# First attention of a two-layer model: VectorE multiplies the keys by their cosine straight from the PSUM banks, and the pooled keys are transposed and copied later

## The reference, cut to what matters

```
kv = x @ w_kv                                  # 256 x 1024 for each sequence
kv = kv * cos + rotate_half(kv) * sin          # rotary positions, on keys and values alike
local keys = values = layernorm(kv over a head's 64) * lng + lnb
p = softmax(kv @ w_proj over 16 tokens)        # pooling inside 16 segments of 16 tokens
pooled = layernorm(sum(p * kv over a segment)) # 16 pooled keys/values per head
out = softmax(q @ [pooled, local].T, masked) @ [pooled, local]
```

## Time and profile before

| what | value |
|---|---|
| median of 3 runs | 1521.95 us (1512.76 to 1534.51) |
| the profiled execution | 1513.62 us, span 1511.8 us |
| PE busy | 1200.5 us (79%) |
| DVE busy | 931.4 us (62%) |
| ACT busy | 822.3 us (54%) |
| POOL busy | 725.5 us (48%) |

### The profile page before, as it was taken

How to read it: one execution, slowest core, us unless ns; L and a number is a source line. 1 busy time by engine, 2 the same in 40 slices (tenths; PEclk the granted TensorE clock), 3 DMA queues, 4 the chain that set the end, 5 groups by cost and what they waited for, 6 DMA issues and landing times. The chain is left out here.

```text
span 1511.8 us, 30131 instructions
## 1 busy us (share of the span) xinstructions
PE 1200.5 (79%) x9299; PEld 928.5 (61%) x9299; DVE 931.4 (62%) x2122; ACT 822.3 (54%) x2181; POOL 725.5 (48%) x750
## 2 busy tenths in 40 slices
PE   3368988989889993898899899889937887888436
PEld 1245665656656662898899889889913444444336
DVE  4687787787876533744744664764434677776633
ACT  1256777767677771676676666666612443344101
POOL 2646748567485312565566556556653323211223
PEclk8589999989998995999999999999966999899558
DMA  7500000000000003303003000000063445331145
GB/s 221 174 2 3 1 10 3 8 10 0 9 2 8 10 8 127 124 11 125 8 11 120 16 9 10 12 12 7 10 174 81 84 87 104 58 48 21 23 121 152
DMA packets 152775, 76.43 MB, mean 51 GB/s; under 512 B 99992, under 2 KB 143384, under 8 KB 152408
## 3 DMA queue, kind: packets, MB, share of 16 engines
q1 hardware_dynamic: 144696, 66.42, 16.8%
q0 software_dynamic: 3072, 6.31, 1.3%
q10 hardware_dynamic: 4896, 2.36, 0.5%
HBM read 54.77 MB, written 19.76 MB: 49 GB/s over the span
## 5 line engine op out<-in xcount | busy, mean ns | idle before, releaser
L1477 POOL TENSOR_TENSOR hl<-hid,hh 128x256 fp32r<-128x256 f32 x396 | 294.0, 744 | 218.8 <-ACT hh L1454 215.1
L1520 DVE SCALAR_TENSOR_TENSOR hid<-GU,gub,sg 128x256 f32<-128x256 f32 x396 | 190.5, 482 | 194.7 <-ACT sg L1448 123.5
L1348 PE MATMUL GU<-xh,wh 128*128 128x256 f32 x792 | 233.3, 295 | 39.4 <-DVE wl L1496 30.3
L1448 ACT ACTIVATE sg<-GU,gub 128x256 f32<-128x256 f32 x396 | 188.1, 475 | 123.6 <-PE GU L1350 121.7
L1349 PE MATMUL GU<-xl,wh 128*128 128x256 f32 x792 | 225.3, 284 | 0.0
L1350 PE MATMUL GU<-xh,wl 128*128 128x256 f32 x792 | 225.1, 284 | 0.0
L1348 PEld LDWEIGHTS GU<-xh,wh 128*128 128x128 f32 x792 | 152.1, 192 | 49.0 <-issue 27.3
L1454 ACT CAST hh<-hid 128x256 fp32r<-128x256 f32 x396 | 158.2, 399 | 25.8 <-DVE hid L1520 25.3
L1349 PEld LDWEIGHTS GU<-xl,wh 128*128 128x128 f32 x792 | 152.5, 193 | 0.0
L1350 PEld LDWEIGHTS GU<-xh,wl 128*128 128x128 f32 x792 | 152.2, 192 | 0.0
L648 ACT ACTIVATE prob<-prob,rZ 128x272 f32<-128x272 f32 (+1 forms) x256 | 98.9, 462 | 60.6 <-DVE rZ L1021 55.2
(11 more groups left out here) (312 smaller groups left out, 2842.6 us busy)
## 6 DMA issues: line engine op xcount, KB each, us to landing
raw<-in_expert_w SPq DMA_DIRECT2D x4, 2688.0 KB, 12.0
late<-in_w SPq DMA_DIRECT2D x20, 256.0 KB, 6.1
raw<-in_expert_w SPq DMA_DIRECT2D x4, 1152.0 KB, 6.1
list<-zero SPq DMA_DIRECT2D x4, 1024.0 KB, 8.6
modb<-mod_d SPq DMA_DIRECT2D x9, 384.0 KB, 4.3
early<-rel_d SPq DMA_DIRECT2D x1, 3072.0 KB, 13.1
qkv_d<-qkv SPq DMA_DIRECT2D x48, 64.0 KB
early<-in_w SPq DMA_DIRECT2D x12, 256.0 KB, 4.2
```

The source lines that it names most:

```text
L1348: pe.matmul(out, lhs[0], rhs[0], start=start, stop=False, skip_group_check=True)
L1448: act.activation(sg[:, c % BUFS], GU[c % BUFS][:, 0:TT], ACT.Silu, bias=gub[:, GATE, e * CH0 + c:e * CH0 + c + 1]).then_inc(silu, 1)
L1477: pool.tensor_tensor(hl[:, b], hid[:, b], hh[:, b].bitcast(F32), ALU.subtract).then_inc(hid_lo, 1)
L1520: dve.scalar_tensor_tensor(out=hid[:, c % BUFS], in0=GU[c % BUFS][:, TT:2 * TT], scalar=gub[:, UP, e * CH0 + c:e * CH0 + c + 1], in1=sg[:, ...
```

## The change

Bank by bank, DVE now makes the cosine product from PSUM, after ACT has copied the bank, and it is this product that drains the bank. ACT's copy signals a new semaphore `kv_out`, for which DVE and POOL wait. `kvraw` stays as the source of POOL's sine product. The instruction of 1024 columns becomes two of 512. In `hp` 6, DVE does `kv_cosine` of the second tokens first, then `kv_rotate` of the first, then `pooled_keys` (before: pooled keys, rotate, cosine). PE's transpose of the pooled keys moves from ahead of the value products to directly ahead of `kT0, kT1`. The wait of `kv_rotate` for `kv_a` is replaced by one for the drained banks.

```diff
                             if k == 0 and not known_zero(r):
                                 act.wait_ge(kv_r, 2 * r + t - 1)
-                            act.copy(kvraw[:, t, k * 512:(k + 1) * 512], a[:]).then_inc(bank.drained, 1)
+                            act.copy(kvraw[:, t, k * 512:(k + 1) * 512], a[:]).then_inc(kv_out, 1)
...
             def kv_cosine(slot, b, t):
 
+                if not known_zero(b):
+                    dve.wait_ge(wk_done, 2 * b)
+                for k, (bank, a) in enumerate(((bank0, A0), (bank1, A1))):
+                    dve.wait_ge(kv_out, 4 * b + 2 * t + k + 1)
+                    bank.wait_full(dve, f"kv{t}{k}", slot)
+                    dve.tensor_tensor(heads_of(kvr[:, t, k * 512:(k + 1) * 512]), heads_of(a[:]),
+                                      cst("cosk")[:, None, t * DH0:(t + 1) * DH0].broadcast_to([P, H0 // 2, DH0]),
+                                      ALU.mult).then_inc(bank.drained, 1)
+
+            def kv_rotate(slot, b, t):
                 bank0.wait_emptied(dve, f"kv{t}0", slot)
                 bank1.wait_emptied(dve, f"kv{t}1", slot)
-                if not known_zero(b):
-                    dve.wait_ge(wk_done, 2 * b)
-                dve.tensor_tensor(heads_of(kvr[:, t, :]), heads_of(kvraw[:, t, :]),
-                                  cst("cosk")[:, None, t * DH0:(t + 1) * DH0].broadcast_to([P, H0, DH0]),
-                                  ALU.mult).then_inc(kv_a, 1)
-
-            def kv_rotate(b, t):
-                dve.wait_ge(kv_a, 2 * b + t + 1)
                 dve.wait_ge(kv_rot, 4 * b + 2 * t + 2)
...
PE's order:
-                    if early and hp == 6:
-                        gkT_mm(slot, slot + 1)
                     if early and hp == 7:
                         for c in (2, 3):
                             kT_mm(slot, slot + 1, np_, c)
...
                     if early and hp == 6:
+                        gkT_mm(slot, slot + 1)
                         for c in (0, 1):
                             kT_mm(slot, slot + 1, np_, c)
...
DVE's order:
+                    if norm and hp == 6:
+                        kv_cosine(slot, r, 1)
+                        kv_rotate(slot, r, 0)
                     if early and hp == 6:
                         pooled_keys(slot, b, np_)
-                    if norm and hp == 6:
-                        kv_rotate(r, 0)
-                        kv_cosine(slot, r, 1)
...
             def swap_rotate(slot, b, t):
-                bank0.wait_emptied(pool, f"kv{t}0", slot)
-                bank1.wait_emptied(pool, f"kv{t}1", slot)
+                pool.wait_ge(kv_out, 4 * b + 2 * t + 2)
```

More of the change, by code:

```diff
@@ L300, in layer0_attention @@
         ln_rstd = sem("ln_rstd")
-        kv_rot = sem("kv_rot")
-        kv_a = sem("kv_a"); kv_r = sem("kv_r"); kv_mean = sem("kv_mean"); kv_c = sem("kv_c")
+        kv_rot = sem("kv_rot"); kv_out = sem("kv_out")
+        kv_r = sem("kv_r"); kv_mean = sem("kv_mean"); kv_c = sem("kv_c")
         kv_sq = sem("kv_sq"); kv_ss = sem("kv_ss"); kv_norm = sem("kv_norm")
@@ L1064, in slot_program @@
                         choose(slot, l)
+                    if norm and hp == 6:
+                        kv_cosine(slot, r, 1)
+                        kv_rotate(slot, r, 0)
                     if early and hp == 6:
                         pooled_keys(slot, b, np_)
-                    if norm and hp == 6:
-                        kv_rotate(r, 0)
-                        kv_cosine(slot, r, 1)
                     if norm and hp == 7:
-                        kv_rotate(r, 1)
+                        kv_rotate(slot, r, 1)
                         kv_center(r, 0)
```

## The result

| | before | after |
|---|---|---|
| median of the runs, us | 1524.68 (1512.76 to 1534.51, 4 runs) | 1559.87 (1552.09 to 1561.7, 4 runs) |
| profiled execution, us | 1513.6 | 1561.7 |
| span, us | 1511.8 | 1559.9 |
| mean granted clock of PE | 0.896 | 0.876 |

After over before is 1.0234, with a 95% interval of 1.0187 to 1.0281: slower by 2.3%, 35.2 us by the medians. The forecast was +23.3 us. The sign and the mechanism came out as predicted, 1559.87 lies in the range, and the size is 12 us short.

The account below looks back on a forecast made before the run. No engine is full; a ring of short steps bounds the first attention, DVE late in steps 6 and 7. Terms 12.5 + 0.9 + 0.9 + 0.5 + 8.5 = 23.3 us gave 1545.3 us, range 1526 to 1567.

Parts of the forecast that it names:

- The cosine product: DVE, steps 5 and 6: pair from PSUM never stretched, 1.29 us; 0.1 us more in step 5, 2.1 us less in step 6.
- The bank held longer: PE at the router, slots 1 to 5: waits 4.4 us for DVE to drain bank1; step 6 begins 2.6 us late.
- Step 7: PE's second wait, at kT0 for the pooled-key copy, uses up DVE's 2.1 us relief; 2.4 us of lateness remain.
- (c): Rival: clock falls for the whole chain after the router and again after PE's second wait; +45, 1567 us; chance 0.27.
- slot 0: No router; kv10 and kv11 wait for the cosine pair, costing step 6 about 0.5 us; 0.9 us in all.
- slots 1 to 5: Loop slots: 2.5 us of waits each, 12.5 us, plus 1.7 us of low clock each behind the router, 8.5 us.
- Start-up: Before the loop: pooled-key copy 5.9 us later, against gains of 2.1, 1.0 and 2.3; 0.5 us, between -2 and +3.
- slot 6: No cosine; pooled keys' transpose and copy stand between the transposes of the probabilities and kT0: 0.9 us.
- (a): The forecast itself, waits plus low clock in the first attention: +18 to +30 us; chance 0.45.
- (b): Rival: waits as forecast, but PE's clock stays up or falls where PE has slack; +15, 1537 us; chance 0.20.
- (d): Rival: late router covered by DVE's choose, so DVE's relief stands alone; -16 us, 1506 us; chance 0.05.
- (e): Rival: product waits in DVE's queue where nothing gets ready earlier, PE had other slack; about 0, 1522 us; chance 0.03.

Follow-up runs that it names:

- filler: Changed kernel plus 32 PE transposes of a constant into a free bank ahead of the router, slots 1 to 5; 1.0134 to the kernel before, 1539.1 us.
- first_only: Kernel before with only the first tokens' cosine product (step 5) taken from PSUM and draining its banks, old orders; 1.0124, 1538.4 us.
- early_mid: Changed kernel, first rotation behind pooled keys, step 5 product ahead of maxima, step 6 product between maxima and rotated queries; 0.9839 to the kernel before, 1495.2 us.
- order_only: Kernel before with only the change's new order of step 6, products still from ACT's copy in SBUF; 1.0209, 1552.7 us.
- early_sooner: Changed kernel, first rotation behind pooled keys, step 5 product ahead of the maxima, step 6 product left in place; 0.9878 to the kernel before, 1500.7 us.
- keys_sooner: Changed kernel with the first rotation moved behind the pooled keys in step 6; 1.0082 to the kernel before, 1530.0 us.
- second_only: Kernel before with only the second tokens' cosine product (step 6) from PSUM, and the change's order of step 6; 1.0227, 1552.0 us.

## Why the prediction was right in sign and short in size

**The cosine product: right.** All 32 instructions of the changed line, and the add of the rotation, in the changed kernel:

```profile
L818 DVE TENSOR_TENSOR kvr<-A,const x32: 673/680/692, 25.5 to 478.4; 128x512 f32<-128x512 f32 x32
L826 DVE TENSOR_TENSOR kvr<-kvr,kvs x16: 1208/1216/3246, 30.6 to 488.2; 128x1024 f32<-128x1024 f32 x16
```

692 ns at most against 3358 ns before. The Trainium skill's rule (SBUF — State Buffer, Who interferes with whom) that an operation of VectorE with at most one SBUF input is not shut out by GpSimd is borne out by the first row; the add, with two, still goes up to 3246. Three of the 32 start at 59.76, 61.40 and 63.28 us, inside a product of POOL on `V` (L1153, 59.48 to 64.15 us), and take 0.69 us each.

**The bank held longer: right.** Forecast 4.4 us of wait at the router, measured 4.23. The step from the router to the scores of step 6 was 6.2 us by the forecast and is 8.34 (334.58 + 1.07 - 327.31): the difference, 2.1 us, is the low clock. `filler` shows the two parts apart: 2.4 us for the wait, where I had 2.6, and 2.2 for the clock, where I had 1.7. `first_only` has the held bank alone and loses 1.2%, and `early_mid` drains from DVE as well, but promptly, and gains. "Evacuate promptly" is the advice of the Trainium skill (PSUM — Partial Sum Buffer, Summary: rules for kernel authors), with the small size of PSUM as its reason. These runs agree with the advice, but for another reason: the next writer of the bank had the path behind it.

**Step 7, the mis-sized term.** The forecast had the second wait at about 2.6 us, measured 2.47, and it had the copy of the pooled keys 6.5 us after the maxima of step 6 done, measured 6.3. What failed is the next sentence: "`kT0` and `kT1` ... 0.93, scores 1.46", 2.4 us, and with it the sentence against (c), "2.6 us is less than the 3.32 us of rows 6". From 342.06 to 344.17 + 1.91 the same work took 4.0 us, at a clock of 0.63 and 0.52. That is 1.6 us, in slot 0 and slots 2 to 5 (not in slot 1), priced at nothing. It is the second half of rival (c). The first half of (c), 3.1 us behind the router, did not come in slots 2 to 5 (2.1), but it did in slot 1, where the clock stays at 0.50 from 191 to 199 us and `filler` takes 3.7 us away. My own sign for it, "if the clock is low at the scores of step 7, (c)", was met, at about two thirds of its price of 2.4. Of the 9.1 us that slots 1 to 5 are off, this is some 6 (step 7 was to be 0.2 us early in each, and is 5.5 late over the five); some 3 are in step 6, the router's clock, 2.2 for 1.7, and slot 1, where 6.0 was lost and not 4.8.

From 23.3 to 38.1 in terms: 9.1 in slots 1 to 5 (30.1 against 21.0), 3.0 in slot 0 (3.9 against 0.9; its sum, 138.1 - 137.28, is 0.8), 2.8 elsewhere. In slot 0 some 1.9 of the 3.0 are in step 7, from its maxima of step 6 to those of step 7 (11.2 us for the 9.3 of the forecast), where PE waits 2.50 us at `kT0` and has a clock of 0.50 behind it. The rest is a step 5 that is 1.3 us late; `order_only` has it too (1.6), without any held bank, and `early_sooner` has not (0.1); its cause is open.

**Elsewhere: a term that was missing.** Of the 5.1 us in step 2, 2.7 are in slot 1. The forecast had no such term, and no row shown there hints at one. See the last section.

**Start-up and slot 6: right in the totals**, 0.5 and 0.8. In slot 6 the mechanism is the forecast's: PE waits 0.80 us at `kT0`. In the start-up the hit is in part luck, since the sum had large terms of both signs (5.9 against 5.4) and errors in them cancelled. POOL's product on `V` (L1153), no longer beside DVE's cosine product, took 4.67 us for 5.62, which is the forecast's 1.0. But POOL was 2.0 us ahead before it already (59.48 for 61.52), a term that the sum does not have. So the add starts 3.0 us sooner (70.76 for 73.76), the copy of the pooled keys is 2.9 us late and not 5.9 (74.09 for 71.19), and the two terms left gave 2.4 us together and not 4.4. `keys_sooner` confirms the large positive term: with the pooled keys ahead of the rotation, the start-up goes from +0.5 to -5.0.

**The rivals.** The forecast itself, (a), ended at +30, and the sign "slots of the loop 2.5 to 5 us longer" with it: the loop's slots are 6.0 to 7.8 us longer. The measured 35 to 38 us lie between (a) and the +45 of (c), and the change that was put inside 2% with 0.67 measured 2.3%. (b), waits without clock, is out: the clock is 0.50 behind the router. (d), a faster kernel, and (e), no effect, are out by the new idle time of DVE ahead of the maxima of steps 6 and 7. That DVE's relief is real, 2 us or so per slot, fits step 7 of `keys_sooner` and `early_mid`, where PE's wait at `kT0` is short; both have another order on DVE too, so it is not measured by itself.

**What the total is made of.** By their totals the halves do not add: the router's half alone +15.3, the second half alone +28.8, together +38.1 and not 44. In the steps that the change touches they do. Steps 6 and 7 of slots 1 to 5 lose 17.0 us in `first_only` (25.1 in step 6, 8.2 given back in step 7), 12.9 in `second_only`, and 30.1 in the whole change. The 6 us between lie elsewhere: 3.2 in step 2 of slots 1 to 6, 2.8 in slot 6, 1.0 in slot 0, less 1.0 in other places. So step 7 costs 1.3 us per slot in the whole change and 2.7 by itself, which fits the 1.3 to 1.7 us that a late step 6 gives back there in `first_only`.

## What to carry to other kernels

When the reader that frees a PSUM bank is moved to another engine, look up where it stands in that engine's queue and what the next writer of the bank has behind it; the product itself may be faster, and the kernel still slower by the queue in front of it (+2.3% here, -1.6% with the same products moved into idle time). Price a new wait of PE twice, once for the wait and once for the same work behind it at half clock; at the router the second part (2.2 us) was nearly as large as the first (2.4). Read from the clock of the trace whether it fell: the length of the wait did not tell here (next section). If one edit carries a reorder, run the reorder alone: here it lost as much as the whole.

## What was not expected of the hardware

- A wait of 2.47 us was enough for the clock to fall from 2.4 to 1.2 GHz behind it, at 0.63 and 0.52 for the 4 us after 342 us, after 6 us of which PE had been busy for 3.59; in slot 0 the same followed a wait of 2.50 us. In `early_mid` a wait of 1.45 us at the same place was followed by a full clock. But the length of the wait alone does not decide. In slot 1 of the changed kernel the clock stayed full behind 2.50 us, and in slot 2 of `early_sooner` it fell behind waits of 1.00 and 0.71 us and took 1.4 us of step 7. The row of the first, then those of the second:

```profile
207.49 1.06 PE L471 MATMUL A<-const,V 128*128 128x128 f32 x8 [2.50 <-DVE kT L912]
```

```profile
242.13 0.44 PE L462 MATMUL A<-const,gk 128*128 128x128 f32 x2 [1.00 <-DVE kvr L818]
243.28 1.31 PE L471 MATMUL A<-const,V 128*128 128x128 f32 x8 [0.71 <-DVE kT L912]
...
244.00:246.00 2.00, 2.00 (x10) 0.50 0.06 12
```

- A stretch of low clock that costs little can move to where it costs. Before, in slot 3, the clock was low around step 0 (the first row below has PE, PEld, DVE, ACT and POOL, then the clock). DVE idled 0.45 and 0.66 us for PE there, and had the maxima of step 1 at 275.0 us without a wait:

```profile
264.00:269.00 5.00, 5.00 (x22) 3.83 (x21) 3.84 (x13) 2.53 (x7) 1.42 (x2) 0.51 0.01 2
```

  In `second_only`, slot 3, it is low from step 1 on and in step 2, where the maxima wait for PE's queries and scores, and step 2 is 3.2 us late:

```profile
274.00:283.00 9.00, 6.27 (x48) 1.00 0.05 15
283.00:293.00 10.00, 9.42 (x37) 0.52 0.05 15
```

  No line of that step was changed. Such a loss of 2.4 to 3.3 us appears in step 2 of one to five of slots 1 to 6 in nine of the eleven changed kernels, faster ones too (3.1 in slot 4 of `early_mid`), and not in `first_only` and `early_sooner`. It goes with the clock each time: in these 20 steps the granted clock between the maxima of step 1 and of step 2 was 0.56 to 0.59, and in the 46 others of slots 1 to 6 it was 0.82 to 1.00, with a loss of 1.0 us at most. What decides in which slot it falls is not settled; that PE's activity ahead of it is shifted by earlier edits is only argued.
- The untouched stages after the attention took between 961 and 976 us over the profiled executions. That is not explained, and it is why the totals of profiled executions were not compared.
